# Vision tower kernel on one core: low and high parts of the last feed-forward piece at other half blocks, and the router's last steps behind the sixth gate product

## What is computed

```python
probs = softmax(x @ router_w)
gates, idx = top_k(probs, 2)
gates = gates / sum(gates)
dense_g = sum(one_hot(idx, 8) * gates[..., None], axis=-2)
g = silu(einsum('bsd,edh->bseh', x, w_gate))
u = einsum('bsd,edh->bseh', x, w_up)
expert_out = einsum('bseh,ehd->bsed', g * u, w_down)
routed = einsum('bse,bsed->bsd', dense_g, expert_out)
shared = silu(x @ ws_gate) * (x @ ws_up) @ ws_down
alpha = sigmoid(x @ sg_w + sg_b)
return alpha * shared + (1.0 - alpha) * routed
```

## Time and profile before

| | |
|---|---|
| median of three runs | 147.86 us (147.77 to 148.08) |
| profiled execution | 147.91 us, span 145.9 us |
| TensorE matmul | 134.5 us busy, 92% of the span |
| VectorE | 105.1 us, 72% |
| ScalarE | 86.2 us, 59% |
| GpSimd | 50.9 us, 35% |
| TensorE clock granted | 0.997 of full speed |

### The profile page before, as it was taken

One profiled execution on the slowest core, in us unless ns is written; L12 is line 12 of the kernel. 1 busy time (PEld: TensorE's weight loads), 2 busy tenths in 40 slices (PEclk: granted clock), 3 DMA queues, 4 the chain that ended last, 5 costly groups with the idle time before them and its releaser, 6 DMA issues.

```text
span 145.9 us, 3999 instructions
## 1 busy us (share of the span) xinstructions
PE 134.5 (92%) x1556; PEld 105.6 (72%) x1556; DVE 105.1 (72%) x268; ACT 86.2 (59%) x206; POOL 50.9 (35%) x72
## 2 busy tenths in 40 slices
PE   7768999999999999997899999998999999999991
PEld 2327679884676787985578788886887888888890
DVE  5499996899977978899876999838666224224453
ACT  0668769640488887883889756566553344344430
POOL 8149000500000000000025334785777577477330
PEclk9999999999999999999999999999999999999998
DMA  4999993078002233007993000368980000000003
GB/s 120 399 366 391 317 344 59 0 233 360 0 7 66 50 92 71 0 4 242 393 404 154 0 0 10 96 181 229 257 231 13 0 4 0 0 0 4 2 0 125
DMA packets 10580, 19.05 MB, mean 131 GB/s; under 512 B 2886, under 2 KB 6290, under 8 KB 10562
## 3 DMA queue, kind: packets, MB, share of 16 engines
q1 hardware_dynamic: 10218, 18.48, 39.3%
q10 hardware_dynamic: 344, 0.32, 0.8%
HBM read 17.84 MB, written 0.96 MB: 129 GB/s over the span
## 4 chain that ended last, share of the span: by engine, by line
PE 64%; DVE 14%; ACT 8%; DMA 5%; issue 4%; POOL 2%; SPq 1%; DVEq 0%; POOLq 0%
PE PS L828 25%; PE PS L858 12%; DMA xs<-in_x_inner_dram 5%; DVE we L1265 4%; PE PS L587 4%; PE PS L626 3%; PE PS L714 3%; PE PS L680 2%; PE PS L695 2%; DVE vhl L1579 2%; DVE xhl L1243 2%; POOL vhl L1200 2%; PE PS L670 1%; PE PS L506 1%; PE PS L569 1%
## 5 line engine op out<-in xcount | busy, mean ns | idle before, releaser
L1209 POOL TENSOR_TENSOR kq<-vhl,kq 128x296 f16<-128x296 f32 x35 | 28.2, 806 | 65.7 <-ACT kq L1116 65.7
L1579 DVE SCALAR_TENSOR_TENSOR vhl<-PS,vhl 128x296 f32<-128x296 f32 x36 | 16.8, 465 | 21.1 <-POOL vhl L1200 13.7
L1109 ACT ACTIVATE vhl<-PS 128x296 f32<-128x296 f32 x36 | 15.0, 415 | 25.6 <-PE PS L828 25.5
L1116 ACT ACTIVATE kq<-vhl 128x296 f16<-128x296 f32 x36 | 16.0, 445 | 4.2 <-DVE vhl L1579 4.2
L1200 POOL TENSOR_TENSOR vhl<-vhl,xs 128x296 f32<-128x296 f32 x14 | 12.5, 895 | 6.8 <-issue 6.0
L828 PE MATMUL PS<-XAh,slab 128*128 128x296 f16 x48 | 10.0, 290 | 0.7 <-DVE vhl L1579 0.7
L828 PE MATMUL PS<-XAh,piece 128*128 128x296 f16 x48 | 9.5, 289 | 1.0 <-ACT XAh L996 0.7
L1265 DVE SCALAR_TENSOR_TENSOR we<-slab,gbs,we 128x192 f32<-128x192 f32 x24 | 9.0, 445 | 1.6 <-ACT we L917 1.6
L828 PE MATMUL PS<-XAh,xsq 128*128 128x296 f16 x48 | 10.0, 289 | 0.0
L506 PE MATMUL PS<-whl,xhl 128*128 128x192 f16 (+1 forms) x40 | 9.9, 247 | 0.0
L508 PE MATMUL PS<-whl,xhl 128*128 128x192 f16 (+1 forms) x40 | 9.9, 246 | 0.0
(11 more groups left out here) (242 smaller groups left out, 363.9 us busy)
## 6 DMA issues: line engine op xcount, KB each, us to landing
slab<-in_w_inner_dram SPq DMA_DIRECT2D x3, 960.0 KB, 9.0
xs<-gate_rows_dram SPq DMA_DIRECT2D x8, 296.0 KB, 8.2
xs<-in_x_inner_dram SPq DMA_DIRECT2D x3, 592.0 KB, 10.0
stage<-in_f_a_dram SPq DMA_DIRECT2D x2, 768.0 KB, 4.9
stage<-in_f_b_dram SPq DMA_DIRECT2D x2, 768.0 KB, 6.4
stage<-gate_rows_dram SPq DMA_DIRECT2D x8, 148.0 KB, 7.3
stage<-in_f_d_dram SPq DMA_DIRECT2D x2, 576.0 KB, 7.1
xhl<-in_f_a_dram SPq DMA_DIRECT2D x1, 768.0 KB, 8.6
```

The lines of the kernel that those rows point to most:

```text
L1109: A(silu[:, i % 2, :], gate_up(i, 0), ACT.Silu, scale=1.0 / XW).then_inc(S["a_silu"], 1)
L1116: A(ah[:, f % ABUF, half * HALF:(half + 1) * HALF], hf[:, i % 3, :], ACT.Copy).then_inc(S["a_ah"], 1)
L1209: G.tensor_tensor(al[:, f % ABUF, cols], hf[:, i % 3, :], ah[:, f % ABUF, cols], ALU.subtract).then_inc(S["g_al"], 1)
L1579: V.scalar_tensor_tensor(out=hf[:, i % 3, :], in0=gate_up(i, 1), scalar=SH / XW, in1=src[:, i % 2, :], op0=ALU.mult, op1=ALU.mult).then_in ...
```

## The change

On ScalarE the six high parts of piece 2 are made at half blocks 8, 9, 10, 11, 12 and 13 (before 8, 10, 12, 14, 16 and 18). On VectorE its six low parts are made at half blocks 10, 11, 13, 14, 19 and 20 (before 10, 12, 13, 17, 18 and 19). gate_split goes from behind product(4) to behind product(5), ahead of gate_values. No operation is added or taken away.

```diff
+LOW_STEPS = (10, 11, 13, 14, 19, 20)
...
                 if 2 <= i < 8:
                     ffn_high(1, i - 2)
-                if i in range(8, 20, 2):
-                    ffn_high(2, (i - 8) // 2)
+                if 8 <= i < 14:
+                    ffn_high(2, i - 8)
...
                 if i == 4:
                     choose_second()
+                if i == 5:
                     gate_split()
-                if i == 5:
                     gate_values()
                 if 5 <= i < 11:
                     ffn_low(1, i - 5)
-                if i in (10, 12, 13, 17, 18, 19):
-                    ffn_low(2, (10, 12, 13, 17, 18, 19).index(i))
+                if i in LOW_STEPS:
+                    ffn_low(2, LOW_STEPS.index(i))
```

## The result

The changed kernel takes **146.72 us** (median of five runs, 146.66 to 146.78) against 147.86 (147.76 to 148.16): a ratio of 0.9913, 95% interval 0.99 to 0.9927. The forecast was 147.05, range 146.4 to 147.4.

The account below looks back on a forecast made before the run. TensorE, busy 92% of the span, was taken as the bound, so only its stops could be won. Terms -0.64 - 0.63 + 0.67 - 0.41 + 0.18 + 0.03 gave -0.80: 147.05 us, range 146.4 to 147.4.

Parts of the forecast that it names:

- Front, 0.64: Router's last steps behind product 5: the matmul stop at half block 7 goes, 0.49, and the gate transposes' wait, 0.15.
- not kept: Rival: VectorE's product 7 or 9 becomes late by what the front won; gain under 0.3, 147.6 to 147.9, chance 0.07.
- High parts, 0: ScalarE's copies at half blocks 8 to 13 fall into gaps: cost 0, at most 0.83 less the gap.
- gu(15), 0.63 gone: TensorE's matmuls of half block 15: their 0.63 stop goes with a low part at 11 in place of 12.
- gu(17), 0.67 of a new stop: TensorE's matmuls of half block 17 wait 0.67 behind product 15, from the low part at 14 and GpSimd's turn.
- The 64-row kind: Low parts starting at partition 64 start later and take longer, 0.24 of the stop at half block 17; otherwise some 0.43.
- gu(21), 0.41 gone: TensorE's matmuls of half block 21: their 0.41 stop goes once no low part stands at 18.
- gu(23), 0.18 of a new stop: TensorE's matmuls of half block 23 stop 0.18 if GpSimd's subtraction goes ahead of the pair product of 21.
- the 0.03 that half block 11 was to cost: VectorE's low part at half block 11 was to delay the gate of 12 by 0.03.
- Moved lows hide wholly: Rival: no turn lost at half blocks 14 and 20; gain 1.68, 146.2 us; chance 0.2 shared with a half-hidden case.
- Only the front gains: Rival: the stop at half block 21 returns in full at 23, low parts 19 and 20 being adjacent; 147.3 us, chance 0.16.
- slower: Rival: VectorE loses the port for three turns of 0.6 at half blocks 13 to 15; 148.3 us, chance 0.03.

Follow-up runs that it names:

- The run without GpSimd's turn: Against the changed kernel, GpSimd's subtraction for half block 14 was held back until VectorE's product of 15 was done: 146.42 us, ratio 0.9894 to the kernel before.
- The run with the order changed: Against the changed kernel, piece 2's high and low parts were made in order 0, 1, 4, 5, 2, 3, the 64-row ones last: 147.04 us.
- the run with the memset: Against the changed kernel, a one-column VectorE memset was put between the low part at half block 20 and the pair product of 21: 147.22 us.
- the run of the lists alone: Against the changed kernel, gate_split was put back behind product(4), so only piece 2's high and low parts moved: 147.57 us, ratio 0.9976 to the kernel before.

## Why the prediction was right, and where its sizes were off

The direction, the places and the mechanism held; the gain was 1.13 where the sum had 0.80.

- **Front, 0.64:** right. gu(7) lost its 0.49 and the transposes their 0.15; alone this part of the change gave 0.64 between down(0) and down(1). L1541 lasts 0.35 now, since it is issued later and still ends with GpSimd's subtraction; L1555 lasts 0.20, no longer 0.68. Product(7) ended at 85.95 and gu(9) started on pitch at 86.60, which is more cover than the 0.4 worked out, so the rival "not kept" fell.
- **High parts, 0:** right, by their own run.
- **gu(15), 0.63 gone:** right. Product(13) had to start at 98.05 in the times of before, that is 97.25 when 0.64 and the 0.16 by which this execution began earlier are taken off; it starts at 97.25.
- **gu(17), 0.67 of a new stop:** mechanism right, size 0.57. The step that failed is "So L1570(15) ends near 102.54": the low part's successor starts at 101.52 and, as the row used there says, lasts 0.90 with GpSimd's turn in it, which makes 102.42. I added the turn and the product's own time separately, which comes out a tenth too high. The run without GpSimd's turn shows its 0.42 alone.
- **The 64-row kind:** the prediction put 0.24 on its later start and longer distance, and 0.43 on the stop if all parts were of the other kind. The run with the order changed has 0.17 there; but 128x576 parts are shorter besides, so it does not isolate the 0.24. Starts 0.50 behind a product and 0.99 to the next recur in every run.
- **gu(21), 0.41 gone:** right; putting a low part back at 18 brought back 0.40 there.
- **gu(23), 0.18 of a new stop:** wrong in this kernel, and the larger part of the miss. The step is "It asks first, so I take 0.18": GpSimd's row begins at 112.01 and VectorE's at 112.02, and VectorE went first. Where GpSimd went first, in the run with the memset, a stop of 0.17 appears, so the price was right and the winner wrong. A difference of 0.05 worked out from rows was not good enough to call it, and the trace of before had the same meeting at 111.61 with VectorE as the winner, which the prediction does not use.

The corrections are 0.18 for the tie and 0.10 for gu(17); with the 0.03 that half block 11 was to cost and did not, the sum is 1.11, against 1.13. Both misses lay on the same side. "Moved lows hide wholly" fell because of gu(17), but it is what the version with the low part at 17 reaches: 1.68 was forecast for that case, its stretch gives 39.80 - 38.12 = 1.68. "Only the front gains" and "slower" fell with the run of the lists alone, whose stretch is 0.51 shorter.

## What to carry to other kernels

Where two engines exclude each other, a filler operation costs nothing only if it fits between the moment its own engine is free and the moment at which either engine must start its next urgent work; read both lists. Idle time behind the filler on its own engine is a hint and no more: in the kernel before the low part at 12 had 0.76 of it behind it (the product at 98.78 in the earlier trace rows) and still made the stop of 0.63, because it stood across the start of GpSimd's gated(13), while in the changed kernel the low part at 20 (111.24) has none behind it and made no stop. The same low part cost 0.57 at half block 14 and nothing at 17. When an order written by hand ends in a near tie, don't count on its outcome: move the work until the margin is more than a few hundredths.

## What was not expected of the hardware

The near ties. Where VectorE's pair product follows a 128x576 low part back to back and GpSimd's subtraction comes at the same moment, the order of the start times does not tell who goes first. In the changed kernel a GpSimd row that begins 0.01 us earlier waits (112.01 against 112.02, 1.07 long); with 17 the first time both have 112.17, and it waits. In the run of the lists alone it begins 0.02 earlier and waits as well:

```profile
112.90 1.08 POOL L1210 TENSOR_TENSOR kq<-vhl,kq 128x296 f16<-128x296 f32 x1 [0.52 <-ACT kq L1117]
112.92 0.45 DVE L1571 TENSOR_TENSOR vhl<-vhl,stage 128x296 f32<-128x296 f32 x1
```

and so it does with 17 the second time (112.46 against 112.48). But in two runs one that begins 0.02 earlier goes first (112.11 against 112.13, and 100.16 against 100.18 in the run with the order changed, 0.75 long). The Trainium skill (SBUF — State Buffer, Who interferes with whom) says, of VectorE's two-port modes, that whoever issues first gets the shared pair for the whole instruction. For the instructions here, with two inputs in SBUF, the traces show nearly the same: gated(13) of before, from 97.15 to 98.69, does its own 0.81 only in the last part, from about 97.88, while the low part's row ends at 98.02. As to who is first, a difference of 0.02 us or less between the start times in a profile does not settle it.
